# A mixture-of-experts layer: GpSimd's cast of the second weights put ahead of its scatter-adds, and gelu biases read without a copy

## The chip, the core and the metric

One core of a Trainium2 chip. The time is the device time of one execution in microseconds, the median over runs; lower is better. The core has engines that run side by side, each with its own queue of instructions in order: TensorE (PE, matmul), VectorE (DVE), ScalarE (ACT), GpSimd (POOL) and SyncE (SP, which here only issues loads and stores). They meet at semaphores.

## What is computed

A small adapter turns x with weights chosen by a condition, then a mixture of 8 experts, top 2 of 8, runs over T = 1024 tokens of 256 values with 160 places per expert and choice, and a shared expert is added:

```
xt = einsum('bct,bcd->bdt', x, w[conditions]).reshape(T, 256)
top_p, top_i = top_k(softmax(xt @ gate_w), 2)
for k in range(2):
    buf[e, pos] = xt                          # pos = place in expert e, dropped at 160 and over
    h = gelu(buf @ w1 + b1)                   # 256 -> 1024, per expert
    y = h @ w2 + b2 + gelu(buf @ wd) @ wu     # 1024 -> 256, and rank 32
    out += y[e, pos] * w[:, None]
out += 0.2 * (gelu(xt @ sw1 + sb1) @ sw2 + sb2 + gelu(xt @ swd) @ swu)
result = x + out.reshape(B, S, D)
```

## The kernel before

Float32 products are made of three matmuls in the fast fp32r type: every operand is split into a high part (a cast) and a low part (the value less the high part), and `three` multiplies high with high and high with low both ways. So all weights and activations pass through a cast on ScalarE or GpSimd and a subtraction on VectorE.

The kernel has a head (condition, gate, routing, shared expert, up to about 80 us) and then eight experts, one period each. Both choices of an expert are done together: its rows (320 places, 288 of them multiplied) lie in a scratch tensor `slot_rows`, filled by scatter (line 423). For expert e:

- **TensorE**: `hidden`, tiles 0 (rank 32) to 8, into three PSUM banks; after tile 2 (tile 1 for the last expert) `turn_results` of expert e-1; then `turn_slots` of expert e+1 (line 970), then `expert_out` (the last expert: `last_out`).
- **ScalarE**: two gelus for each tile (lines 526, 527), w1's casts for expert e+1, the turned slots' high part, half of w2's casts (line 470), the copies of y (line 561).
- **VectorE**: the low part of each tile (line 623); behind tile 2 the last chunk, chunk 3, of `w2_l` of expert e (line 599); behind tile 3 (tile 1 for the last expert) `weigh_rows` of expert e-1 into `y_row` (line 740), which first waits until the scatter-adds of expert e-2 have landed (`combined`), as `y_row` is there only once; then w1's low parts for e+1 (line 587), `wd` and `wu`, the slots' low part, chunks 0 to 2 of `w2_l`.
- **GpSimd**, `period` (line 428), the queue that is changed: `small_hi(e + 2)` casts `wd` and `wu` (lines 358, 363); `combine(e - 1)`, three scatter-adds of `y_row` into `out` (line 401); `side_data(e)`, five small operations that give the slots' weights `slot_w`, which `weigh_rows` reads, and target rows (lines 380 to 389), signalled by `slots_sided`; `set_bias(e + 1)` copies 8 columns of `bias_t` to `bias_now` (line 374); `w2_hi_part(e + 2)` casts chunks 2 and 3 of w2 (line 369), when its load has landed. Weights are numbered v = e + 1, since number 0 is the shared expert: `e + 2` in the code is the next expert's weights.
- **SyncE**, its queue strictly in order (lines 307 to 310): `load_first(e + 1)` w1, wd, wu, b2 once the raw ones are used; `load_slots(e)`, which waits for `slots_turned` and for `slots_sided` of the expert two before it, as `slot_in` has two buffers; `load_second(e + 1)` w2 (line 265), which waits until `w2_lo` has used all of `w2_raw`, of which there is one buffer.

Routing, shared expert and the loops of other engines are as printed.

Of the kernel before, what the change touches and what calls it, by code (L numbers as in the profile page):

```python
# [15 lines left out]
P = 128  # L16
# [4 lines left out]
E, K = 8, 2  # L21
# [3 lines left out]
SLOTS = K * CAP  # L25
SHARED_SCALE = 0.2
KD = D // P
NF = H // P
# [21 lines left out]
def build(nc, x, itok, cond_w, gate_w, w1, b1, w2, b2, wd, wu, sw1, sb1, sw2, sb2, swd, swu, out, slot_rows, cond_rows):  # L50
    with ExitStack() as ctx:
        def sb(name, shape, dt=F32):
            return ctx.enter_context(nc.sbuf_tensor(name, shape, dt))
# [4 lines left out]
        def sem(name):  # L58
            return ctx.enter_context(nc.semaphore(name))
# [31 lines left out]
        gate2 = sb("gate2", [P, KD, 2 * E], F32R)  # L91
        bias_rows = sb("bias_rows", [P, P])
        bias_t = sb("bias_t", [P, N_BIAS])
        bias_now = [sb(f"bias_now{i}", [P, NF]) for i in range(2)]
        less_high = sb("less_high", [P, 1])
        empty_row = sb("empty_row", [P, ROW])

# [52 lines left out]
        spare_out = sem("spare_out")  # L150
        dispatched = sem("dispatched")
        base_out = sem("base_out")
# [21 lines left out]
        scores_copied = sem("scores_copied")  # L174
        bias_turned = sem("bias_turned")
        bias_ready = sem("bias_ready")
        bias_set = sem("bias_set")
        route = sem("route")
        centred = sem("centred")
        expd_made = sem("expd_made")  # L180
# [19 lines left out]
        y_copied = sem("y_copied")  # L200
# [25 lines left out]
        def hid_count(u, j):  # L226
            return u * HT + (j + 1)
# [7 lines left out]
        def hid_bank(u, j):  # L235
            return hid_ring(u)[j % len(hid_ring(u))]
# [83 lines left out]
        def _(pool):  # L320
# [31 lines left out]
            def small_hi(v, par, waits=True):  # L352

                if waits:
                    pool.wait_ge(hid_made, hid_before(v))
                pool.wait_ge(wd_in, 16 * (v + 1))
                for g in range(3):
                    ins = pool.tensor_copy(wd_h[par][:, :, g, :], wd_raw[:, :, :])  # L358
                ins.then_inc(wd_hi, 1)
                if waits:  # L360
                    pool.wait_ge(y_made, y_before(v))
                pool.wait_ge(wu_in, 64 * (v + 1))
                pool.tensor_copy(wu_s[par][:, :], wu_raw[:, :]).then_inc(wu_hi, 1)

            def w2_hi_part(v, par):

                pool.wait_ge(w2_in, 16 * (v + 1))
                for c in range(ACT_W2, CHUNKS):
                    pool.tensor_copy(w2_h[par][:, c * FT:(c + 1) * FT, :],  # L369
                                     w2_raw[:, c * FT:(c + 1) * FT, :]).then_inc(w2_hi[1], 1)  # L370

            def set_bias(e, par):

                pool.tensor_copy(bias_now[par][:, :], bias_t[:, e * NF:(e + 1) * NF]).then_inc(bias_set, 1)

            def side_data(e, par):


                pool.wait_ge(slots_in[par], (e + (2 - par)) * 16)
                pool.tensor_copy(slot_w[par][:, :], slot_in[par][:, :, W_COL]).then_inc(slot_math, 1)  # L380
                pool.tensor_scalar(slot_free[:, :], slot_in[par][:, :, ID_COL], float(T), None,
                                   ALU.is_ge).then_inc(slot_math, 1)
                pool.wait_ge(slot_math, e * SIDE + 2)
                pool.tensor_tensor(slot_spare[:, :], slot_free[:, :], slot_local[:, :], ALU.mult).then_inc(slot_math, 1)
                pool.wait_ge(slot_math, e * SIDE + 3)
                pool.tensor_tensor(slot_row[:, :], slot_spare[:, :], slot_in[par][:, :, ID_COL],
                                   ALU.add).then_inc(slot_math, 1)
                pool.wait_ge(slot_math, e * SIDE + 4)
                pool.tensor_copy(slot_tok[par][:, :], slot_row[:, :]).then_inc(slots_sided, KD)

            def combine(e, par):

                pool.wait_ge(y_weighted, e * ST + 1)
                pool.wait_ge(slots_sided, (e + 1) * KD)
                if e > 0:
                    pool.wait_ge(combined, e * (16 * ST))
                for s in range(ST):
                    n = ST_ROWS[s]
                    if s > 0:
                        pool.wait_ge(y_weighted, e * ST + s + 1)  # L400
                    pool.indirect_dma_start(  # L401
                        out=out, out_offset=bass.IndirectOffsetOnAxis(ap=slot_tok[par][0:n, s:s + 1].bitcast(U32), axis=0),
                        in_=y_row[0:n, s, :], in_offset=None, bounds_check=T + SLOTS - 1,
                        compute_op=ALU.add).then_inc(combined, 16)
# [4 lines left out]
            for b in range(NT // 2):  # L409
                pool.wait_ge(rows_copied, b + 1)  # L410
                pool.tensor_copy(token_row[1][:, 2 * b:2 * b + 2, 0:D],
                                 token_row[0][:, 2 * b:2 * b + 2, 0:D]).then_inc(rows_twice, 1)
            pool.wait_ge(bias_ready, 1)
            set_bias(0, 0)
            small_hi(1, 1, waits=False)

            pool.wait_ge(rows_copied, NT // 2)
# [7 lines left out]
                        in_=token_row[k][:, t, :], in_offset=None, bounds_check=E * SLOTS - 1,  # L425
                        oob_is_err=False).then_inc(dispatched, 16)

            def period(e, par, combine_one=True, split=True, biases=True):
                if split:
                    small_hi(e + 2, par)  # L430
                if combine_one:
                    combine(e - 1, 1 - par)
                side_data(e, par)
                if biases:
                    if combine_one:
                        pool.wait_ge(y_copied, e * KD)
                    set_bias(e + 1, 1 - par)
                if split:
                    w2_hi_part(e + 2, par)

            period(0, 0, combine_one=False)
            pool.wait_ge(base_out, 32)
            pool.wait_ge(spare_out, 16)
            for e in range(1, E - 1):
                period(e, e % 2)
            period(7, 1, split=False, biases=False)
            combine(7, 1)


        @block.scalar  # L450
        def _(act):
# [5 lines left out]
            def w1_chunk(v, par, c):  # L457

                if c == 0:
                    act.wait_ge(w1_in, 16 * (v + 1))  # L460
                act.activation(w1_h[par][:, :, c * FC:(c + 1) * FC], w1_raw[:, :, c * FC:(c + 1) * FC],  # L461
                               ACT.Copy).then_inc(w1_hi, 1)

            def w2_chunk(v, par, c):

                if c == 0:
                    act.wait_ge(w2_in, 16 * (v + 1))
                    if v >= 2:
                        act.wait_ge(y_made, y_before(v))
                act.activation(w2_h[par][:, c * FT:(c + 1) * FT, :], w2_raw[:, c * FT:(c + 1) * FT, :],  # L470
                               ACT.Copy).then_inc(w2_hi[0], 1)
# [42 lines left out]
            def gelu_tile(u, j, n, bias):  # L514

                act.wait_ge(hid_made, hid_count(u, j))
                if u == 0 and j < 3:
                    pass
                else:
                    act.wait_ge(hid_split, hid_count(u, j) - 3)  # L520
                src = hid_bank(u, j)
                if j == 0:
                    act.activation(gelu_f[2 * RANK:3 * RANK, 0, 0:n], src[2 * RANK:3 * RANK, 0:n], ACT.Gelu)
                    act.activation(low_s[0:LOW, 0:n], src[0:LOW, 0:n], ACT.Gelu).then_inc(hid_gelu, 1)
                else:
                    act.activation(gelu_f[:, j % 3, 0:n], src[:, 0:n], ACT.Gelu, bias=bias(j - 1))  # L526
                    act.activation(hid_h[:, j - 1, 0:n], src[:, 0:n], ACT.Gelu, bias=bias(j - 1)).then_inc(hid_gelu, 1)  # L527

            def slots_hi_part():
                for k in range(KD):  # L530
                    act.activation(xs_h[:, k, :], turn_ps[k][:, 0:SLOTS], ACT.Copy).then_inc(slots_hi, 1)
# [11 lines left out]
            slots_hi_part()  # L543

            def period(e, par, split=True, turned=True):

                act.wait_ge(bias_set, e + 1)

                for j in range(HT):
                    gelu_tile(e + 2, j, SLOTS, lambda f: bias_now[par][:, f:f + 1])  # L550
                if split:
                    for c in range(CHUNKS):
                        w1_chunk(e + 2, par, c)
                        if c == 1:
                            act.wait_ge(slots_turned, e * KD + 2 * KD)
                            slots_hi_part()
                    for c in range(ACT_W2):
                        w2_chunk(e + 2, par, c)
                for m in range(KD if turned else 0):
                    act.wait_ge(y_made, 2 * HTILES + (e * KD + (m + 1)))  # L560
                    act.activation(y_t[:, m, :], y_ps[m][:, 0:SLOTS], ACT.Copy).then_inc(y_copied, 1)

            period(0, 0)
            for e in range(1, E - 1):
                period(e, e % 2)
            period(7, 1, split=False, turned=False)


# [481 lines left out]
```

## Time and profile before

| | us |
|---|---|
| median of 3 runs | 210.36 (210.09 to 210.44) |
| the profiled execution | 210.76 |
| its span, first to last instruction | 208.9 |

| engine | busy us | share of the span |
|---|---|---|
| TensorE | 191.0 | 91% |
| VectorE | 134.4 | 64% |
| ScalarE | 132.9 | 64% |
| GpSimd | 112.0 | 54% |

Times inside a trace are microseconds from the start of the span. A timeline row gives start, length, engine, line, operation, what it writes and reads, and in brackets how long the engine was idle before it and what ended that. A waits row gives who waited for whom. "Issue" is time in which an engine waited for nothing that the profile shows.

### The profile page before, as it was taken

The numbers are of one execution on the slowest core, as the hardware profiler recorded it, in microseconds if no ns is written. First come the engines' busy times: TensorE is split into PE (matmuls) and PEld (weight loads), VectorE is DVE, ScalarE is ACT, GpSimd is POOL, SyncE is SP. The second block draws the span as 40 slices with busy tenths as digits, with TensorE's granted clock in tenths as the row PEclk, the third lists the DMA queues.
The fourth block names the chain that finished last, engine by engine and source line by source line (L and its number), as shares of the span: only waits on it lengthen the run. The fifth ranks groups of instructions, "written<-read, shape, count | busy, mean of one in ns | idle before, by whom it ended". The sixth has DMA issues, their size and how long they took to land.

```text
span 208.9 us, 3977 instructions
## 1 busy us (share of the span) xinstructions
PE 191.0 (91%) x1409; PEld 183.1 (88%) x1409; DVE 134.4 (64%) x294; ACT 132.9 (64%) x283; POOL 112.0 (54%) x162
## 2 busy tenths in 40 slices
PE   6569999999999499999999999999999999999930
PEld 6567777998888499999999999999999999999920
DVE  4547489744852024695878869869869968968020
ACT  2247799903890106968949949949949859768000
POOL 6202304087872015001784894885876867948662
PEclk9969999999999799999999999999999999999995
DMA  5599972422221895017867867866787776600523
GB/s 178 166 300 321 221 259 50 173 80 78 102 100 57 222 350 183 3 20 275 224 107 237 218 147 217 209 194 198 171 232 202 129 258 220 90 1 6 60 32 38
DMA packets 27898, 33.04 MB, mean 158 GB/s; under 512 B 4554, under 2 KB 24772, under 8 KB 27876
## 3 DMA queue, kind: packets, MB, share of 16 engines
q1 hardware_dynamic: 23748, 27.31, 42.8%
q0 software_dynamic: 3760, 4.89, 14.4%
q10 hardware_dynamic: 368, 0.56, 0.9%
q8 instruction: 13, 0.21, 0.4%
q14 instruction: 9, 0.07, 0.1%
HBM read 23.96 MB, written 8.79 MB: 157 GB/s over the span
## 4 chain that ended last, share of the span: by engine, by line
POOL 28%; PE 24%; issue 19%; DVE 16%; DMA 8%; POOLq 1%; ACT 1%; SPq 1%; DVEq 0%
POOL out_rows L401 13%; POOL slot_w L380 6%; POOL slot_rows L423 5%; DVE w_l L599 5%; DVE y_row L740 4%; PE hid_ps L806 3%; PE hid_ps L808 3%; PE hid_ps L807 3%; DVE hid_l L623 3%; DMA gate_raw<-in_L_ffn_gate_w 2%; PE y_ps L806 2%; PE y_ps L808 2%; PE y_ps L807 2%; DMA out_rows<-y_row,slot_tok 2%; DMA slot_rows<-token_row,slot_i 2%
## 5 line engine op out<-in xcount | busy, mean ns | idle before, releaser
L401 POOL DMA_INDIRECT out_rows<-y_row,slot_tok x24 | 46.0, 1919 | 14.3 <-DVE y_row L740 6.7
L623 DVE TENSOR_TENSOR hid_l<-gelu_f,hid_h 128x320 fp32r<-128x320 f32 (+1 forms) x80 | 41.3, 531 | 13.6 <-ACT hid_h L527 12.7
L806 PE MATMUL hid_ps<-xs_h,w_h 128*128 128x288 f32 x128 | 38.2, 298 | 0.0
L808 PE MATMUL hid_ps<-xs_h,w_l 128*128 128x288 f32 x128 | 37.6, 294 | 0.0
L807 PE MATMUL hid_ps<-xs_l,w_h 128*128 128x288 f32 x128 | 37.6, 294 | 0.0
L526 ACT ACTIVATE gelu_f<-hid_ps,bias_now 128x320 f32<-128x320 f32 x64 | 35.0, 547 | 1.1 <-PE hid_ps L808 0.4
L527 ACT ACTIVATE hid_h<-hid_ps,bias_now 128x320 fp32r<-128x320 f32 x64 | 35.4, 553 | 0.0
L358 POOL CAST wd_h<-wd_raw 128x64 fp32r<-128x64 f32 x27 | 9.9, 404 | 45.8 <-DMA wd_raw<-in_L_ffn_wd 44.7
L599 DVE TENSOR_TENSOR w_l<-w_raw,w_h 128x512 fp32r<-128x512 f32 x36 | 26.3, 748 | 12.5 <-POOL w_h L369 11.8
L808 PE MATMUL y_ps<-hid_h,w_l 128*128 128x288 f32 x112 | 32.9, 294 | 0.0
L807 PE MATMUL y_ps<-hid_l,w_h 128*128 128x288 f32 x112 | 32.9, 294 | 0.0
L806 PE MATMUL y_ps<-hid_h,w_h 128*128 128x288 f32 x112 | 32.9, 294 | 0.0
L423 POOL DMA_INDIRECT slot_rows<-token_row,slot_i x16 | 17.9, 1121 | 11.8 <-issue 11.8
L807 PEld LDWEIGHTS hid_ps<-xs_l,w_h 128*128 128x128 f32 x128 | 24.0, 188 | 0.0
L806 PEld LDWEIGHTS hid_ps<-xs_h,w_h 128*128 128x128 f32 x128 | 24.0, 188 | 0.0
L808 PEld LDWEIGHTS hid_ps<-xs_h,w_l 128*128 128x128 f32 x128 | 24.0, 188 | 0.0
L587 DVE TENSOR_TENSOR w_l<-w_raw,w_h 128x512 fp32r<-128x512 f32 x36 | 23.4, 685 | 0.5 <-ACT w_h L461 0.3
L806 PE MATMUL y_ps<-w_h,hid_h 128*128 128x256 f32 x80 | 23.0, 287 | 0.0
L808 PE MATMUL y_ps<-w_h,hid_l 128*128 128x256 f32 x80 | 22.9, 286 | 0.0
L807 PE MATMUL y_ps<-w_l,hid_h 128*128 128x256 f32 x80 | 22.9, 286 | 0.0
L461 ACT ACTIVATE w_h<-w_raw 128x512 fp32r<-128x512 f32 x36 | 22.0, 702 | 0.0
L806 PEld LDWEIGHTS y_ps<-hid_h,w_h 128*128 128x128 f32 x112 | 21.0, 188 | 0.0
(182 smaller groups left out, 422.5 us busy)
## 6 DMA issues: line engine op xcount, KB each, us to landing
w_raw<-in_L_ffn_w SPq DMA_DIRECT2D x16, 1024.0 KB, 5.3
slot_rows<-empty_row SPq DMA_DIRECT2D x1, 2600.0 KB, 17.1
slot_in<-slot_rows SPq DMA_DIRECT2D x8, 260.0 KB, 3.7
x_in<-in_x SPq DMA_DIRECT2D x2, 512.0 KB, 4.4
w_raw<-in_L_ffn_sw SPq DMA_DIRECT2D x1, 1024.0 KB
out_rows<-base SPq DMA_DIRECT2D x2, 512.0 KB, 3.6
wu_raw<-in_L_ffn_wu SPq DMA_DIRECT2D x24, 32.0 KB
slot_in<-slot_rows SPq DMA_DIRECT2D x8, 65.0 KB, 3.8
```

What stands on the lines that cost most here:

```text
L380: pool.tensor_copy(slot_w[par][:, :], slot_in[par][:, :, W_COL]).then_inc(slot_math, 1)
L401: pool.indirect_dma_start(out=out, out_offset=bass.IndirectOffsetOnAxis(ap=slot_tok[par][0:n, s:s + 1].bitcast(U32), axis=0), in_=y_row[0: ...
L423: pool.indirect_dma_start(out=slot_rows, out_offset=bass.IndirectOffsetOnAxis(ap=slot_i[:, t, k:k + 1].bitcast(U32), axis=0), in_=token_ro ...
L461: act.activation(w1_h[par][:, :, c * FC:(c + 1) * FC], w1_raw[:, :, c * FC:(c + 1) * FC], ACT.Copy).then_inc(w1_hi, 1)
L526: act.activation(gelu_f[:, j % 3, 0:n], src[:, 0:n], ACT.Gelu, bias=bias(j - 1))
L527: act.activation(hid_h[:, j - 1, 0:n], src[:, 0:n], ACT.Gelu, bias=bias(j - 1)).then_inc(hid_gelu, 1)
L587: dve.tensor_tensor(w1_l[par][:, :, cols], w1_raw[:, :, cols], w1_h[par][:, :, cols].bitcast(F32), ALU.subtract).then_inc(w1_lo, 1)
L599: dve.tensor_tensor(w2_l[par][:, rows, :], w2_raw[:, rows, :], w2_h[par][:, rows, :].bitcast(F32), ALU.subtract).then_inc(w2_lo, 1)
L623: dve.tensor_tensor(hid_l[:, j - 1, 0:n], gelu_f[:, j % 3, 0:n], hid_h[:, j - 1, 0:n].bitcast(F32), ALU.subtract).then_inc(hid_split, 1)
L806: pe.matmul(out_ap, l_h, r_h, start=start, stop=False)
L807: pe.matmul(out_ap, l_h, r_l, start=False, stop=False)
L808: return pe.matmul(out_ap, l_l, r_h, start=False, stop=stop)
```

## The change

GpSimd's period is put in another order: small casts, w2's casts, then scatter-adds, then side data. The waits on the first store of `out` stand ahead of the scatter-adds of period 1 as before, but behind that period's casts. `set_bias`, `bias_now` and `bias_set` go: the gelus read `bias_t` directly, and ScalarE no longer waits at a period's start, nor GpSimd for `y_copied`.

```diff
@@ gpsimd
-            pool.wait_ge(bias_ready, 1)
-            set_bias(0, 0)
             small_hi(1, 1, waits=False)
@@
-            def period(e, par, combine_one=True, split=True, biases=True):
-                if split:
+            def period(e, par):
+                if e + 2 <= E:
                     small_hi(e + 2, par)
-                if combine_one:
+                    w2_hi_part(e + 2, par)
+                if e == 1:
+                    pool.wait_ge(base_out, 32)
+                    pool.wait_ge(spare_out, 16)
+                if e > 0:
                     combine(e - 1, 1 - par)
                 side_data(e, par)
-                if biases:
-                    if combine_one:
-                        pool.wait_ge(y_copied, e * KD)
-                    set_bias(e + 1, 1 - par)
-                if split:
-                    w2_hi_part(e + 2, par)
...
+            for e in range(E):
                 period(e, e % 2)
-            period(7, 1, split=False, biases=False)
-            combine(7, 1)
+            combine(E - 1, (E - 1) % 2)
@@ scalar
-                act.wait_ge(bias_set, e + 1)
                 for j in range(HT):
-                    gelu_tile(e + 2, j, SLOTS, lambda f: bias_now[par][:, f:f + 1])
+                    gelu_tile(e + 2, j, SLOTS, lambda f: bias_t[:, e * NF + f:e * NF + f + 1])
```

## Rows read from the trace of the kernel before

**Rows 1.** Page, section 1: busy us (share of the span) and instructions

```profile
PE 191.0 (91%) x1409; PEld 183.1 (88%) x1409; DVE 134.4 (64%) x294; ACT 132.9 (64%) x283; POOL 112.0 (54%) x162
```

**Rows 2.** Windows, the fifth period: busy of each engine, clock, DMA share, GB/s

```profile
127.70:142.70 15.00, 15.00 (x118) 15.00 (x117) 12.23 (x28) 12.16 (x29) 11.40 (x16) 1.00 0.74 196
```

**Rows 3.** Waits: engine and line waited for releaser: us in total, times, longest

```profile
DVE w_l L599 <- POOL w_h L369: 11.8, 6, 2.0
...
ACT gelu_f L523 <- POOL bias_now L374: 4.5, 6, 0.8
```

**Rows 4.** Chain of waits, last 22 us: start, length, what

```profile
194.44 4.25 DMA out_rows<-y_row,slot_tok
```

**Rows 5.** Timeline of GpSimd, one period: start, length, line, operation

```profile
172.85 1.21 POOL L358 CAST wd_h<-wd_raw 128x64 fp32r<-128x64 f32 x3 [2.09 <-DMA wd_raw<-in_L_ffn_wd]
...
174.99 2.31 POOL L401 DMA_INDIRECT out_rows<-y_row,slot_tok  x1 [0.59 <-DVE y_row L740]
...
179.71 1.69 POOL L401 DMA_INDIRECT out_rows<-y_row,slot_tok  x1 [0.31 <-issue]
180.89 2.45 POOL L380 COPY slot_w<-slot_in 128x3 f32<-128x3 f32 x1
...
184.35 0.19 POOL L389 CAST slot_tok<-slot_row 128x3 int32<-128x3 f32 x1
...
184.62 1.16 POOL L369 CAST w_h<-w_raw 128x512 fp32r<-128x512 f32 x2
```

**Rows 6.** Timeline of VectorE, same period and the end of it

```profile
172.67 0.69 DVE L599 TENSOR_TENSOR w_l<-w_raw,w_h 128x512 fp32r<-128x512 f32 x1
...
176.65 0.49 DVE L623 TENSOR_TENSOR hid_l<-gelu_f,hid_h 128x320 fp32r<-128x320 f32 x1 [0.34 <-ACT hid_h L527]
...
182.01 1.29 DVE L599 TENSOR_TENSOR w_l<-w_raw,w_h 128x512 fp32r<-128x512 f32 x2
185.26 1.07 DVE L599 TENSOR_TENSOR w_l<-w_raw,w_h 128x512 fp32r<-128x512 f32 x1 [1.96 <-POOL w_h L369]
...
187.28 0.48 DVE L740 TENSOR_SCALAR y_row<-y_ps,slot_w 128x256 f32<-128x256 f32 x1
```

**Rows 7.** Timeline of SyncE's queue, from 64 to 174 us: start, length, what

```profile
97.97 0.38 SPq L265 DMA_DIRECT2D w_raw<-in_L_ffn_w  x1
...
169.86 0.38 SPq L272 DMA_DIRECT2D slot_in<-slot_rows  x1
170.29 0.48 SPq L273 DMA_DIRECT2D slot_in<-slot_rows  x1
173.38 0.39 SPq L265 DMA_DIRECT2D w_raw<-in_L_ffn_w  x1
```

**Rows 8.** Windows of half a microsecond, behind the load of 173.38

```profile
177.50:178.00 0.50, 0.50 (x6) 0.50 (x5) 0.47 (x2) 0.50 (x2) 0.39 (x1) 1.00 1.13 305
178.00:178.50 0.50, 0.50 (x6) 0.50 (x5) 0.50 (x1) 0.50 (x2) 0.50 (x1) 1.00 1.03 115
```

**Rows 9.** Timeline of GpSimd, narrow windows: single small casts

```profile
172.85 0.60 POOL L358 CAST wd_h<-wd_raw 128x64 fp32r<-128x64 f32 x1 [2.09 <-DMA wd_raw<-in_L_ffn_wd]
...
173.84 0.23 POOL L358 CAST wd_h<-wd_raw 128x64 fp32r<-128x64 f32 x1
```

**Rows 10.** Timeline of GpSimd, end of the kernel

```profile
188.55 3.72 POOL L401 DMA_INDIRECT out_rows<-y_row,slot_tok  x1 [2.77 <-DVE y_row L740]
...
197.08 0.18 POOL L389 CAST slot_tok<-slot_row 128x3 int32<-128x3 f32 x1
199.99 1.66 POOL L401 DMA_INDIRECT out_rows<-y_row,slot_tok  x1 [2.73 <-DVE y_row L750]
...
203.81 1.43 POOL L401 DMA_INDIRECT out_rows<-y_row,slot_tok  x1 [0.30 <-issue]
```

**Rows 11.** Timeline of TensorE, turning of the next slots

```profile
176.08 0.82 PE L970 MATMUL turn_ps<-ident,slot_in 128*128 128x128 f32 x6
```

**Rows 12.** Line 272, load of slots: us from issue to landing

```profile
DMA to landing us min/median/max: 2.7/3.7/3.8
```

More of the change, by code:

```diff
@@ L93, in build @@
         bias_t = sb("bias_t", [P, N_BIAS])
-        bias_now = [sb(f"bias_now{i}", [P, NF]) for i in range(2)]
         less_high = sb("less_high", [P, 1])
@@ L176, in build @@
         bias_ready = sem("bias_ready")
-        bias_set = sem("bias_set")
         route = sem("route")
@@ L370, in w2_hi_part @@
                                      w2_raw[:, c * FT:(c + 1) * FT, :]).then_inc(w2_hi[1], 1)
-            def set_bias(e, par):
-                pool.tensor_copy(bias_now[par][:, :], bias_t[:, e * NF:(e + 1) * NF]).then_inc(bias_set, 1)
             def side_data(e, par):
@@ L426, in _ @@
                         oob_is_err=False).then_inc(dispatched, 16)
-            def period(e, par, combine_one=True, split=True, biases=True):
-                if split:
+            def period(e, par):
+                if e + 2 <= E:
                     small_hi(e + 2, par)
-                if combine_one:
+                    w2_hi_part(e + 2, par)
[3 more added lines that the diff above has]
+                if e > 0:
                     combine(e - 1, 1 - par)
                 side_data(e, par)
-                if biases:
-                    if combine_one:
-                        pool.wait_ge(y_copied, e * KD)
-                    set_bias(e + 1, 1 - par)
-                if split:
-                    w2_hi_part(e + 2, par)
[L441 to L444, printed above, removed]
+            for e in range(E):
                 period(e, e % 2)
-            period(7, 1, split=False, biases=False)
-            combine(7, 1)
+            combine(E - 1, (E - 1) % 2)
         @block.scalar
```

## The prediction, made before the changed kernel ran

> **What bounds the kernel now.** I read the page's busy times first: TensorE is at work for 191.0 us of a span of 208.9 [rows 1]. A share over the whole span hides stages, so next came the windows by stage: in an expert's period, 15.0 us long and repeated from 97.7 to 187.3, TensorE is busy for 15.00 of 15.00 us, while VectorE has 12.23, ScalarE 12.16 and GpSimd 11.40 [rows 2]. Inside a period there is nothing to win for any other engine. The table of waits names the two things that the change is aimed at: VectorE waits for GpSimd's cast of the second weights, 11.8 us in 6 waits, and ScalarE for `bias_now`, 4.5 us in 6 [rows 3]. Both waits lie beside a TensorE that never stops for them, so their 16.3 us are no part of the span. The chain of waits does run through GpSimd; that chain starts at the end, and in the periods it only shows who was released last, not that TensorE waited.
>
> Time can be won only behind 187.3, where the chain is real: `y_row` of expert 6 is weighed at 187.28 (W7 below), three scatter-adds follow, the last starts at 194.44, its rows land 4.25 us later, `y_row` is written again for expert 7, three more scatter-adds, the end [rows 4, 6, 10].
>
> **The biases.** Removed: eight copies of 128x8, about 0.2 us each (as the cast of `slot_tok` of that size [rows 5]), and ScalarE's wait. A gelu reads the same [128,1] column from `bias_t` instead of `bias_now`; same form, cost 0. ScalarE starts each period up to 0.8 us earlier [rows 3], under TensorE's cover: gain 0 in the periods, at most those 0.8 us in the last one, if W7 hung on it.
>
> **The cast moved ahead.** In a period GpSimd now does: `wd`/`wu` casts, three scatter-adds, side data, bias copy, two casts of `w2` [rows 5]. After: small casts, wait for `w2_raw`, two casts, scatter-adds, side data. The load of `w2_raw` goes out only when VectorE has used the old one (its chunk 3 ends at 173.36, the load is issued at 173.38 [rows 6, 7]), only 1.6 us ahead of the first scatter-add at 174.99 [rows 5]. So the casts cannot come early: everything queued behind them on GpSimd (scatter-adds, side data) now waits for a transfer that had been hidden.
>
> I count from the issue L of that load:
> - L to landing 5.0 us: the 1 MB issued at 173.38 holds the DMA queues at 305 GB/s up to 178.0, then the rate falls to 115 [rows 8]. Bounds 4.8 and 5.5 (slots are issued right ahead of it now).
> - two casts, 2.0 us. Undisturbed they take 1.16 [rows 5]. They would start in VectorE's run of subtractions (w1 chunks, from about L+4.6). There a 128x64 cast took 0.60 against 0.23 us a moment later, as if it waited for the end of one VectorE instruction each [rows 9]; with two such waits of some 0.4 us, 2.0. Bounds 1.2 and 2.5.
> - first to third scatter-add, start to start: 4.7 us (174.99 to 179.71). Bounds 3.8 (199.99 to 203.81, all quiet) and 5.9 (188.55 to 194.44) [rows 4, 5, 10].
> - third scatter-add's start to the end of the side data: 4.8 us in a period (179.71 to 184.54), 2.8 at the end of the kernel where VectorE is idle (194.44 to 197.26) [rows 4, 5, 10]. In the new place VectorE goes through an expert's first tiles, 0.49 us each with some 0.3 us of waiting between them, as in [rows 6]: 3.3, nearer the quiet row.
> - side data to next L: 0.9 us. SyncE's queue is in order: `load_slots` waits for `slots_sided`, and `load_second` stands behind it. Its two issues start at 169.86 and 170.29, the second takes 0.48 [rows 7].
>
> Sum: 5.0 + 2.0 + 4.7 + 3.3 + 0.9 = 15.9 us from one L to the next, a closed loop over SyncE and GpSimd. It is longer than TensorE's 15.0. Before, the loop had no 5.0 and no 2.0 in it, because the scatter-adds did not wait for the load. That is what this change turns from hidden work into the bound.
>
> How it adds up: L1 is 97.97. Then L2 = 97.97 + 15.9 = 113.87 (now 113.36, one period of 15.0 before the next), and L6 = 113.87 + 4 x 15.9 = 177.47, against 173.38 [rows 7]. The scatter-adds of expert 5 then start at 184.5, the third at 189.2, and land 4.25 later at 193.4. W7 waits for that landing (`combined`), since `y_row` is single. Before, this landing was at 179.7 + 4.25 = 184.0 and W7 at 187.28 hung on other things. So W7 moves by 6.1 us.
>
> From W7 to the end I keep the 21.6 us of before. It holds a first scatter-add of 3.72 us against 2.31 in the periods [rows 5, 10]; it may shrink by up to 1.4, it doesn't grow. TensorE's own last work follows W7, as VectorE's remaining tiles stand behind the weighing.
>
> **Who notices on the way.** `load_slots` is now issued by the late side data. TensorE turns the slots 2.7 us after L now (176.08 against 173.38 [rows 7, 11]); the slot load is issued 0.9 before L and lands 3.7 us (2.7 to 3.8) after its issue [rows 12], the second one 0.4 later, so at about L+3.2. TensorE therefore stands 0.5 us plus L's delay in the first period and then once per period about what the loop has over 15.0. This is the same delay, not a second one. The granted clock is 1.00 in the periods [rows 2], the 2.4 GHz level; I take no change of it for gaps of a microsecond.
>
> What is removed is then: VectorE's 1.96 us wait for the cast goes (11.8 in all), ScalarE's wait goes, and neither is worth anything.
>
> **The rivals.**
> 1. The tail alone. If casts, scatter-adds and side data take their quiet values, the loop is 4.8 + 1.2 + 3.8 + 2.8 + 0.9 = 13.5, under 15.0: no period grows. L6 stays 173.38 and the landing of expert 5 comes 4.8 + 1.2 + 3.8 + 4.25 = 14.05 to, with a loop just at 15.0, 15.2 us later, at 187.4 to 188.6; W7 is late by 0.1 to 1.3 us. Time 210.5 to 211.7, taken as 211.2. For it: the wait frees VectorE of a 1.07 us subtraction that ran beside the cast [rows 6]. Against: no period shows quiet values for all three.
> 2. Faster. VectorE no longer waits for the cast at 185.26, so W7 could be up to 0.8 us earlier (as ScalarE's first tile), if expert 5's rows have landed by 186.5, which means 13.1 us after L6. The quiet sum is 14.05. It needs each value below its lowest row: 209.6 to 210.2. Likewise "it does nothing": 210.4.
> 3. The casts are held by the whole VectorE run, not by one instruction. The copy of `slot_w` behind the third scatter-add ended at 183.34, after 2.45 us, and VectorE's unbroken run at 183.30, while a copy of that size takes 0.2 [rows 5, 6]. If that holds for the casts, they start at about L+9.9 (183.30 against 173.38) and the loop is 11.1 + 4.7 + 3.3 + 0.9 = 20.0: L6 = 197.97, landing at 218.0, W7 later by 30.7 us, 241 us. Against: the small casts in [rows 9], which got through one at a time.
> The Trainium skill's GPSIMD Engine Reference, section Key points, says that GpSimd shares its SBUF interfaces with VectorE and contends with VectorE instructions that have two SBUF inputs. It doesn't say how long GpSimd is kept out; taken as full exclusion it gives rival 3, about 241 us, and taken as sharing in turn it gives the forecast. The rows on casts agree with turns, the row on `slot_w` with exclusion.
>
> **How the numbers follow.** Forecast 72%: 210.36 + 6.1, rounded to 216.5 us. The profiled execution took 210.76, its span is 208.9, 1.86 outside it; it is 0.4 above the median of the runs, and I add to the median. Its own range: with a loop of 15.3, L6 = 174.5 and W7 = 189.9 (+2.6, 213.0); with 17.0, L6 = 183.0 and landing at 199.8 (+12.5, 222.9). Rival 1: 12%. Rival 2 with no effect: 10%, half of it faster. Rival 3 and everything over 223: 6%. The low end takes in most of rival 1: 211.0 to 222.9. A measurement here can tell about 0.2% from no change; faster 0.05, same 0.06, slower 0.89.
>
> **What would show it.** Right: GpSimd's cast of `w2` waits for the DMA of `w_raw` some 4 us in each of six periods; VectorE's `y_row` waits for the landing of `out_rows` in periods 3 to 7; TensorE waits for `slot_in`; L265 is issued about 15.9 us apart. Wrong in size: casts of 0.6 us each, or L265 still 15.0 apart (rival 1), or casts that end with VectorE's run (rival 3). Wrong altogether: the scatter-adds start within 3 us of L, or the last `y_row` of expert 6 is at 187 or before.

## The result: slower, by the loop that was forecast, and twice as far

The changed kernel takes 223.18 us (median of four runs, 222.38 to 228.71) against 210.4 us of the kernel before, measured beside it: ratio 1.0622, 95% interval 1.0566 to 1.0679. The forecast was 216.5 us with a range up to 222.9; sign and mechanism were right, the size was not. In this document medians are over all runs of a kernel and ratios over its fast ones alone, as some executions take a few us more at a lower granted clock.

The profiled execution of the changed kernel (called after in what follows) took 222.38 us, its span is 220.5. The page, busy times and the first groups:

```profile
span 220.5 us, 3969 instructions
PE 194.7 (88%) x1409; PEld 185.4 (84%) x1409; DVE 136.6 (62%) x294; ACT 134.6 (61%) x283; POOL 101.2 (46%) x154
...
L367 POOL CAST w_h<-w_raw 128x512 fp32r<-128x512 f32 x14 | 11.8, 871 | 38.3 <-DMA w_raw<-in_L_ffn_w 38.3
```

Against [rows 1], GpSimd has 10.8 us less work and TensorE 3.7 us more; the span is 11.6 us longer. No engine got busier by that much: the time is waiting. The last line says whose: GpSimd stood 38.3 us in front of the casts, for the load of raw w2. The table of waits of after (who waited for whom: us, times, longest), beside [rows 3]:

```profile
POOL w_h L367 <- DMA w_raw<-in_L_ffn_w: 38.3, 7, 7.2
...
PE turn_ps L953 <- DMA slot_in<-slot_rows: 10.7, 6, 2.9
...
DVE y_row L723 <- DMA out_rows<-y_row,slot_tok: 6.7, 5, 2.9
...
SPq L269 <- POOL slot_tok L383: 23.6, 5, 6.4
```

The two waits that the change was aimed at are gone. In their place are the load in front of the casts, TensorE in front of its slots, `y_row` in front of its landing, and SyncE's queue, which waits for the side data in five periods. SyncE's timeline shows what comes of it (start, length, line; L253 is w1, L270 and L271 are the slots, L263 is w2):

```profile
99.21 0.39 SPq L263 DMA_DIRECT2D w_raw<-in_L_ffn_w  x1
109.25 0.37 SPq L253 DMA_DIRECT2D w_raw<-in_L_ffn_w  x1
...
114.65 0.38 SPq L270 DMA_DIRECT2D slot_in<-slot_rows  x1
115.07 0.48 SPq L271 DMA_DIRECT2D slot_in<-slot_rows  x1
115.59 0.60 SPq L263 DMA_DIRECT2D w_raw<-in_L_ffn_w  x1
...
132.76 0.59 SPq L263 DMA_DIRECT2D w_raw<-in_L_ffn_w  x1
...
149.35 0.58 SPq L263 DMA_DIRECT2D w_raw<-in_L_ffn_w  x1
...
166.84 0.59 SPq L263 DMA_DIRECT2D w_raw<-in_L_ffn_w  x1
...
183.95 0.59 SPq L263 DMA_DIRECT2D w_raw<-in_L_ffn_w  x1
```

From the first to the last L263 it is 84.74 us for five periods, 16.95 each; before it was 173.38 - 97.97 = 75.41, 15.08 each [rows 7]. One period on GpSimd's timeline:

```profile
122.75 1.63 POOL L367 CAST w_h<-w_raw 128x512 fp32r<-128x512 f32 x2 [6.33 <-DMA w_raw<-in_L_ffn_w]
124.55 1.90 POOL L395 DMA_INDIRECT out_rows<-y_row,slot_tok  x1 [0.17 <-issue]
126.75 1.56 POOL L395 DMA_INDIRECT out_rows<-y_row,slot_tok  x1 [0.30 <-issue]
128.62 1.43 POOL L395 DMA_INDIRECT out_rows<-y_row,slot_tok  x1 [0.30 <-issue]
129.54 0.70 POOL L374 COPY slot_w<-slot_in 128x3 f32<-128x3 f32 x1
...
131.55 0.19 POOL L383 CAST slot_tok<-slot_row 128x3 int32<-128x3 f32 x1
```

The load issued at 115.59 lets the casts start at 122.75; at 131.74 the side data ends; at 131.81 SyncE issues the slots, at 132.76 the next w2. The loop is closed, as the chain of the prediction has it.

Where the 11.6 us of span are: the head before the first slot load, whose code is the same but for one copy, took 68.69 us in this execution and 67.34 in that of before (1.35 us). It took 65.7 to 68.7 in the traces of this study, and 65.74 in after_yrow, whose code up to there is that of after, so it is spread and no effect of the change. From the first slot load to L6 it is 9.2 us more, from L6 to W7 1.8 more, from W7 to the end 0.8 less.

### The profile page after: what moved, and what is told of

Read it like the earlier page. It is cut to its first block, busy times and chain, and to the rows that moved or that the text cites. A ratio compares the mean times of both kernels' runs of the same rounds, so it can differ in the third digit from the quotient of the medians.

```text
span 220.5 us, 3969 instructions
## 1 busy us (share of the span) xinstructions
PE 194.7 (88%) x1409; PEld 185.4 (84%) x1409; DVE 136.6 (62%) x294; ACT 134.6 (61%) x283; POOL 101.2 (46%) x154
## 4 chain that ended last, share of the span: by engine, by line
issue 29%; POOL 24%; PE 22%; DMA 12%; DVE 6%; ACT 4%; POOLq 1%; SPq 1%; DVEq 0%
POOL out_rows L395 12%; POOL slot_rows L415 5%; DMA out_rows<-y_row,slot_tok 3%; DMA gate_raw<-in_L_ffn_gate_w 3%; DMA slot_in<-slot_rows 3%; DMA wd_raw<-in_L_ffn_wd 2%; PE y_ps L791 2%; PE y_ps L789 2%; PE hid_ps L789 2%; PE y_ps L790 2%; PE hid_ps L791 2%; PE hid_ps L790 2%; ACT gelu_f L512 2%; POOL wd_h L356 2%; PE hid_ps L810 2%
## 5 line engine op out<-in xcount | busy, mean ns | idle before, releaser
L512 ACT ACTIVATE gelu_f<-hid_ps,bias_t 128x320 f32<-128x320 f32 (+1 forms) x77 | 43.7, 568 | 9.6 <-DVE hid_l L606 4.9
L395 POOL DMA_INDIRECT out_rows<-y_row,slot_tok x24 | 41.1, 1713 | 9.1 <-issue 6.1
L513 ACT ACTIVATE hid_h<-hid_ps,bias_t 128x320 fp32r<-128x320 f32 (+1 forms) x77 | 43.8, 569 | 0.0
L367 POOL CAST w_h<-w_raw 128x512 fp32r<-128x512 f32 x14 | 11.8, 871 | 38.3 <-DMA w_raw<-in_L_ffn_w 38.3
L582 DVE TENSOR_TENSOR w_l<-w_raw,w_h 128x512 fp32r<-128x512 f32 x36 | 25.2, 730 | 1.6 <-ACT w_h L456 1.6
L570 DVE TENSOR_TENSOR w_l<-w_raw,w_h 128x512 fp32r<-128x512 f32 x36 | 25.1, 731 | 0.5 <-ACT w_h L447 0.3
L789 PE MATMUL y_ps<-w_h,hid_h 128*128 128x256 f32 x80 | 23.9, 299 | 0.0
L791 PE MATMUL y_ps<-w_h,hid_l 128*128 128x256 f32 x80 | 23.7, 297 | 0.0
L790 PE MATMUL y_ps<-w_l,hid_h 128*128 128x256 f32 x80 | 23.7, 297 | 0.0
L356 POOL CAST wd_h<-wd_raw 128x64 fp32r<-128x64 f32 x27 | 7.8, 327 | 34.3 <-DMA wd_raw<-in_L_ffn_wd 32.9
L447 ACT ACTIVATE w_h<-w_raw 128x512 fp32r<-128x512 f32 x36 | 21.3, 664 | 0.0
```

What stands on the lines that cost most here:

```text
L395: pool.indirect_dma_start(out=out, out_offset=bass.IndirectOffsetOnAxis(ap=slot_tok[par][0:n, s:s + 1].bitcast(U32), axis=0), in_=y_row[0: ...
L570: dve.tensor_tensor(w1_l[par][:, :, cols], w1_raw[:, :, cols], w1_h[par][:, :, cols].bitcast(F32), ALU.subtract).then_inc(w1_lo, 1)
L582: dve.tensor_tensor(w2_l[par][:, rows, :], w2_raw[:, rows, :], w2_h[par][:, rows, :].bitcast(F32), ALU.subtract).then_inc(w2_lo, 1)
L789: pe.matmul(out_ap, l_h, r_h, start=start, stop=False)
L790: pe.matmul(out_ap, l_h, r_l, start=False, stop=False)
L791: return pe.matmul(out_ap, l_l, r_h, start=False, stop=stop)
```

## The experiments

L is an issue of the w2 load; "period" is the mean distance of the six L from 97 us on, or of the first six weighings of `y_row` where that is said. Each ratio is to the kernel before, run on the same chip, where its median was 209.6 to 210.4.

| run | median us | ratio, 95% interval | period us |
|---|---|---|---|
| changed kernel | 223.18 | 1.062 (1.057 to 1.068) | 16.95 |
| bias_only | 210.06 | 1.003 (0.998 to 1.007) | 15.0 (weighings) |
| order_only | 230.55 | 1.096 (1.089 to 1.104) | 18.2 |
| side_first | 227.05 | 1.074 (1.062 to 1.085) | 17.5 |
| second_first_same_wait | 238.8 | 1.133 (1.126 to 1.140) | 20.3 |
| one_cast_on_act | 220.31 | 1.052 (1.041 to 1.063) | 16.5 |
| casts_on_act | 219.67 | 1.046 (1.039 to 1.055) | 16.6 |
| after_yrow | 221.19 | 1.055 (1.048 to 1.062) | 17.2 |
| side_first_yrow | 213.82 | 1.016 (1.011 to 1.022) | 15.1 |
| w2_double | 208.59 | 0.994 (0.989 to 0.998) | 15.0 (weighings) |
| w2_double_old_order | 209.95 | 0.988 (0.980 to 0.996) | 15.0 (weighings) |
| both_double | 209.1 | 0.994 (0.990 to 0.998) | 15.0 (weighings) |
| yrow_double | 209.94 | 1.000 (0.996 to 1.004) | 15.0 (weighings) |

### Each part by itself

```diff
# bias_only, to the kernel before
-                act.wait_ge(bias_set, e + 1)
-                    gelu_tile(e + 2, j, SLOTS, lambda f: bias_now[par][:, f:f + 1])
+                    gelu_tile(e + 2, j, SLOTS, lambda f: bias_t[:, e * NF + f:e * NF + f + 1])
# order_only, to the kernel before
                     small_hi(e + 2, par)
+                    w2_hi_part(e + 2, par)
...
                     set_bias(e + 1, 1 - par)
-                if split:
-                    w2_hi_part(e + 2, par)
```

> The change's bias part alone: the gelus read bias_t, no copy, no bias_set; GpSimd's old order is kept. Theory (all of the loss is the order of GpSimd's queue): 210.2 us, within 0.2% of before. Rival (the head, which ended 1.2 us later in the changed kernel's profile, or the wider table read by ScalarE, costs something): 211 to 212.

> The change's order alone: casts of w2 ahead of the scatter-adds, bias copies kept behind the side data. Theory: as the changed kernel, 223 us, issues of the w2 load some 17 us apart. Rival (the two parts work together, for instance through the start of ScalarE's tiles): more than 1 us off 223.

The biases alone give 1.003 (0.998 to 1.007): nothing that can be told from no change, as forecast, and no cost of the wider table. The order alone is not 223 but 230.55: the expectation missed by 7 us, on the side of its rival. Waits and SyncE's queue of order_only:

```profile
ACT gelu_f L523 <- POOL bias_now L374: 24.6, 6, 5.4
...
PE hid_ps L806 <- ACT low_s L524: 15.4, 6, 3.8
...
SPq L265 <- DVE w_l L599: 18.8, 7, 3.1
```

```profile
112.26 0.38 SPq L272 DMA_DIRECT2D slot_in<-slot_rows  x1
112.68 0.48 SPq L273 DMA_DIRECT2D slot_in<-slot_rows  x1
116.23 0.39 SPq L265 DMA_DIRECT2D w_raw<-in_L_ffn_w  x1
```

Behind the side data now stands the bias copy, and ScalarE's first tile waits for it (24.6 us in all, against 4.5 in [rows 3]). VectorE's last chunk of w2 stands behind the low part of tile 2, and the next load waits for the chunk (the last of these lines): it goes 4.0 us after the slots (112.26 to 116.23) instead of 0.9. So the biases' part, which alone is worth nothing, is worth some 7 us under the new order: it takes a second wait off the loop. The halves of the change can't be added up from runs of each.

### The link over SyncE

```diff
# second_first_same_wait, to the changed kernel
                 load_first(e + 1)
+                sp.wait_ge(slots_turned, (e - 1) * KD)
+                sp.wait_ge(slots_sided, (e - 1) * KD)
+                load_second(e + 1)
                 load_slots(e, e % 2)
-                load_second(e + 1)
```

> The changed kernel with SyncE's two loads swapped behind the same waits: w2 first, the slots behind it. Theory (the 6 to 7 us from issue to landing of w2, against 5.0 before, come from the slot load right ahead of it in the queue): the casts start 5.0 to 5.4 us after the issue; but the slots then land about 6.2 us after it, TensorE turns them late, and the period becomes some 18.4: 230 us. Rival (the load is slow for another reason): 6 to 7 us still.

The casts start 5.3 to 6.0 us after L (5.5 in the next two lines; mean 5.6), against 6.2 to 7.2 us in periods 2 to 6 of after (mean 6.7). So about 1.1 us of the load's time goes with the slot load that stands right ahead of it in the queue. order_only points the same way: there the slots are issued 3 to 4 us ahead of w2, and the casts start 5.2 to 5.5 us after L. It isn't the whole of it: in side_first, with the slots issued 1.4 to 3.4 us ahead, it took 5.5 to 6.8 us, and two issues with the same lead of 3.1 us took 5.5 and 6.8.

```profile
118.30 0.39 SPq L263 DMA_DIRECT2D w_raw<-in_L_ffn_w  x1
```

```profile
123.77 1.63 POOL L369 CAST w_h<-w_raw 128x512 fp32r<-128x512 f32 x2 [8.03 <-DMA w_raw<-in_L_ffn_w]
```

The slots come late instead, TensorE waits 23.7 us for them in all, and the whole is 238.8, 9 us over the expectation: the periods are 20.3 us, not the 18.4 that it names. A part of that miss is the clock. Windows of the same run (span of the window, busy of TensorE, ..., granted clock, DMA share, GB/s):

```profile
121.50:124.50 3.00, 0.00 (x0) 0.00 (x0) 2.29 (x5) 2.20 (x5) 0.73 (x2) 1.00 0.83 273
125.00:128.00 3.00, 3.00 (x14) 3.00 (x15) 2.34 (x7) 1.66 (x4) 2.53 (x3) 0.51 0.15 13
```

TensorE did nothing for 3.4 us (121.45 to 124.88), and in the 3 us from 125.0 on it was granted 0.51, close to the 1.2 GHz level: 14 matmuls where 3 us hold some 24 at full clock (118 in 15.0 us, [rows 2]).

### The second loop

```diff
# side_first, to the changed kernel
-                if e > 0:
-                    combine(e - 1, 1 - par)
+                if e > 1:
+                    pool.wait_ge(combined, (e - 1) * (16 * ST))
                 side_data(e, par)
+                if e > 0:
+                    combine(e - 1, 1 - par)
```

> The changed kernel with the five side-data operations put between the casts and the scatter-adds (with a wait for scatter-adds that landed long before). Theory (a closed loop: load of w2, casts, scatter-adds, side data, release of the slot load, next load of w2): the loop loses its scatter-adds, 4 us, and falls to some 12, so TensorE's 15.0 decides again; only the last landing stays late, 212 us. Rival (the periods grow because scatter-adds and y_row are late, not because side data is): 218 to 223.

227.05 us: the rival's side, and slower than the changed kernel. The forecast of 212 was wrong. SyncE no longer waits for the side data, and still the periods are long, because a wait that lay beside the first loop now ends last (side_first, the waits):

```profile
DVE y_row L725 <- DMA out_rows<-y_row,slot_tok: 18.3, 6, 6.1
...
ACT gelu_f L514 <- DVE hid_l L608: 16.4, 6, 5.9
```

The side data puts the scatter-adds 3 us further back; they land beside the next 1 MB load (the third one started at 130.46, `y_row` was free at 136.27, 5.8 us later, against 3.1 for the last one of after, 196.58 to 199.67). VectorE stands before `y_row`, behind it the tiles, behind them ScalarE and TensorE. If that is a second loop, two buffers for `y_row` must open it, and in the changed kernel itself they must do little:

```diff
# after_yrow and side_first_yrow: two buffers, the second on the stored base rows
-        y_row = sb("y_row", [P, ST, D])
+        y_rows = [sb("y_row", [P, ST, D]), base[:, 0:ST, :]]
...
-                    dve.wait_ge(combined, e * (16 * ST))
+                    dve.wait_ge(combined, (e - 1) * (16 * ST))
```

> Side data ahead of the scatter-adds, as in side_first (227 us), and two buffers for y_row, so that VectorE doesn't wait for the landing of the last scatter-adds. Theory (side_first opened the loop over the slot load, but a second loop, load of w2, casts, scatter-adds, landing, y_row, TensorE's next tiles, took its place): with both open TensorE's 15.0 us decide and the whole takes 211 us. Rival (only one loop exists, and something else made side_first slow): 218 or more.

> The changed kernel with two buffers for y_row only. Theory (in the changed kernel the loop over side data and the slot load is the one that decides, the wait of y_row lies beside it): periods stay near 17.0 us, only the two weighings at the end leave the chain, 220 to 222 us. Rival (y_row's wait makes the periods long): 216 or less.

Both came out that way. With only `y_row` doubled the changed kernel stays at 17.2 us from L to L (one of the five turns took 19.6, the others 16.4 to 16.7) and 221.19 us. With both loops open the periods are TensorE's again (15.1), and 227.05 falls to 213.82; the 2.8 us over the expected 211 lie in the tail, where from W7 to the end it is 24.7 us against 21.6, as GpSimd comes to the last scatter-adds late. So the changed kernel hangs on the loop over side data and slots, and beside it stands another that would make a period as long (17.5 us in side_first, against 16.95). Opening one of them alone buys 2 us or nothing, opening both buys the periods back.

### Taking links out of the loop

> The changed kernel with three of the four w2 casts on ScalarE, one on GpSimd (before: two and two). Theory (closed loop): each period is one cast shorter, 0.9 us, and the last landing too: 223.2 less 6 times 0.9, about 217.8. Rival (what counts is the wait for the load and what it does to TensorE, not GpSimd's time behind it): 222 to 223.

> The changed kernel with all four w2 casts on ScalarE; GpSimd only keeps the wait for the load ahead of its scatter-adds. Theory: the loop is 6.5 (load) + 4.1 + 3.4 + 1.1 = 15.1, so about TensorE's 15.0, if ScalarE has room for two more casts (1.2 us of some 2 us idle): 212 us. Rival (ScalarE becomes the bound): above 216.

The edit is one number, the count of w2's chunks that ScalarE casts (`ACT_W2 = 2` becomes 3, or 4). One cast less shortened the period by 0.5 us, not 0.9, and two less by 0.4. The total of one_cast_on_act says little: its four runs took 217.85, 219.17, 221.45 and 225.81 us at granted clocks of 0.970, 0.981, 0.960 and 0.953, and the expected 217.8 is near the first two. For casts_on_act it is plain: 219.67 where the theory had 212, on the side of its rival (above 216). The rival's reason, ScalarE as the bound, doesn't hold. The loop still closes over GpSimd, as the means over its five turns show:

| step | after | one_cast_on_act | casts_on_act |
|---|---|---|---|
| L to the first cast, or to the scatter-adds | 6.5 | 6.6 | 7.1 |
| casts | 1.8 | 0.9 | none |
| first to third scatter-add | 4.0 | 4.3 | 5.1 |
| third scatter-add to the end of the side data | 3.6 | 3.7 | 3.4 |
| side data to next L | 1.0 | 1.0 | 1.0 |
| sum | 16.95 | 16.5 | 16.6 |

Most of what the casts gave back went into the wait ahead of the scatter-adds and into the scatter-adds. GpSimd in casts_on_act, and VectorE beside it:

```profile
120.28 4.57 POOL L395 DMA_INDIRECT out_rows<-y_row,slot_tok  x1 [6.42 <-DMA w_raw<-in_L_ffn_w]
...
138.16 3.71 POOL L395 DMA_INDIRECT out_rows<-y_row,slot_tok  x1 [7.29 <-DMA w_raw<-in_L_ffn_w]
```

```profile
121.43 1.90 DVE L582 TENSOR_TENSOR w_l<-w_raw,w_h 128x512 fp32r<-128x512 f32 x3
...
138.46 1.89 DVE L582 TENSOR_TENSOR w_l<-w_raw,w_h 128x512 fp32r<-128x512 f32 x3
```

Without casts in front, the first scatter-add takes up to 4.6 us; behind a cast it took 1.7 to 1.9 in after. The lines show what the long ones have in common. VectorE's unbroken run of subtractions (no gap of 0.15 us in it) ends at 123.33, the scatter-add at 124.85; the next run ends at 140.35, the scatter-add at 141.87: 1.52 us later both times. Over all traces of this study 14 scatter-adds took more than 3 us, and each ended 1.4 to 1.6 us after the end of such a run (in side_first, 4.29 us long, after the last of w2's subtractions in it). So a long one looks like one that is held until VectorE pauses. Which ones are held was not settled: 1.66 and 2.14 us stand in the same run, and no experiment moved VectorE's work away. A link taken out of the loop was so filled for the most part by the next one.

### Taking the load out of the loop

```diff
# w2_double, to the changed kernel; v = 2, 4, 6, 8 lie on the tokens' second copy
-                sp.wait_ge(w2_lo, v * CHUNKS)
-                sp.dma_start(w2_raw[:, :, :], w2_v[v - 1]).then_inc(w2_in, 16)
+                if v == 2:
+                    sp.wait_ge(dispatched, 16 * NT * K)
+                else:
+                    sp.wait_ge(w2_lo, max(v - 1, 1) * CHUNKS)
+                sp.dma_start(w2_src(v)[:, :, :], w2_v[v - 1]).then_inc(w2_ins[w2_buf(v)], 16)
...
+                load_second(e + 1)
                 load_first(e + 1)
                 load_slots(e, e % 2)
-                load_second(e + 1)
```

> The changed kernel with two buffers for the raw w2 (the second one lies on a copy of the tokens that is no longer used) and its load issued at the head of SyncE's turn, almost a period early. Theory (the load between two steps of GpSimd's queue is what closed the loop): the cast waits for nothing, periods of 15.0 us, the cast off VectorE's path at the end: 209.8 us, at most 0.3% under before. Rival (the cast ahead of the scatter-adds costs by its own 1.8 us): 211 to 213.

208.59 us, ratio 0.994 (0.989 to 0.998): the new order with its load a period early is 6.5% faster than with the load in the loop (223.18), and no slower than before. Windows of it:

```profile
157.20:172.20 15.00, 15.00 (x118) 15.00 (x117) 12.23 (x28) 12.20 (x29) 9.70 (x13) 1.00 0.76 195
172.20:184.95 12.75, 12.75 (x101) 12.75 (x101) 10.57 (x25) 9.96 (x23) 9.36 (x13) 1.00 0.24 28
```

TensorE never stops in these periods, as in [rows 2], and of GpSimd's 38.3 us in front of the casts 2.0 are left, in one wait. The casts and their place in the queue are the same as in after, so neither cost the time: the load in front of them did. The second buffer and the earlier issue came together in this edit; what each is worth alone was not run.

What the new order is then worth by itself:

> The old order of GpSimd's queue (casts behind the side data) with gelus from bias_t, two buffers of raw w2 and the early load, as in w2_double (208.6 us). Theory (the early load alone is worth nothing in the old order, where the casts stand behind the scatter-adds; w2_double's gain comes from the casts' new place): 210.0 us, within 0.3% of before. Rival (the gain is the early load's): 208.6.

By the totals this can't be said: 0.988 (0.980 to 0.996) and 0.994 (0.989 to 0.998) overlap, and the first rests on two runs (206.73 and 209.12 us; the other two took 210.77 and 211.6). The forecast of no difference to before isn't borne out by that interval, nor refuted by so few runs. The traces say where to look. From the weighing of expert 5 to the end of the span it is 208.9 - 173.72 = 35.2 us before, 35.3 in bias_only (173.52 to 208.8) and 35.2 in w2_double_old_order (173.73 to 208.9), all with the old order; it is 33.0 in w2_double (172.16 to 205.2) and 33.3 in both_double (175.22 to 208.5), with the new one. In both of these VectorE weighs expert 6 12.8 us after expert 5 (184.95 in w2_double), against 13.6 before and 13.4 in the other two, as its subtraction doesn't wait for the cast; and the first scatter-add behind it takes 2.92 us against 3.72:

```profile
186.22 2.92 POOL L408 DMA_INDIRECT out_rows<-y_row,slot_tok  x1 [3.50 <-DVE y_row L736]
```

So with the early load the new order gives some 2 us, at the tail alone, in two traces against three. The profiled executions differ by more (206.99 us in w2_double, 210.77 in w2_double_old_order) because of the head as well: the first slot load is issued at 65.91 us, behind a granted clock of 1.00, in w2_double, and at 67.53, behind 0.97, in the other.

> The bias part alone plus two buffers for y_row (the second one on the stored base rows). Theory (behind the last period the chain waits for the landing of expert 6's rows before y_row is written again, but the scatter-adds of expert 7 must wait for the same landing and TensorE's last rows come 1.5 us behind it): at most 1.3 us better, 209.0 us. Rival: no difference, as TensorE's last rows decide.

> w2_double plus two buffers for y_row. Theory (its last periods run at TensorE's pace; at the end TensorE's last rows decide): 208.4 us, no more than 0.2% under w2_double, some 0.7% under before. Rival (the wait of y_row is on the chain at the end): 207.3.

Two buffers for `y_row` alone: 1.000 (0.996 to 1.004), the rival; in both_double 0.994 (0.990 to 0.998), the same as w2_double, so neither the 208.4 nor the rival's 207.3 can be told from its 209.1. At the end TensorE's last rows and the landing of expert 6's scatter-adds, for which those of expert 7 must wait anyway, come last. The three kernels with two buffers of raw w2 are the fastest of this study, w2_double by 0.6% over before, and are not told apart by their totals.

## Why the prediction was right in kind and short in size

- **What bounds it**: right. TensorE's 15.0 us hid everything; bias_only confirms that ScalarE's wait was worth nothing, and the removed waits of [rows 3] brought nothing.
- **The load between two steps of GpSimd's queue closes a loop over SyncE**: right, and shown by taking it out (w2_double).
- **The terms of the loop**: means over its five turns in after, and as predicted:

| step | predicted | measured |
|---|---|---|
| L to the start of the casts | 5.0 (4.8 to 5.5) | 6.5 (5.3 to 7.2) |
| casts | 2.0 | 1.8 |
| first to third scatter-add | 4.7 | 4.0 |
| third scatter-add to the end of the side data | 3.3 | 3.6 |
| side data to next L | 0.9 | 1.0 |
| sum | 15.9 | 16.95 |

The step that failed is the first term, "L to landing 5.0 us", bounds 4.8 and 5.5; it measured 6.5. I took the load's time from a load with nothing right ahead of it (the second slot load was issued 3.1 us before it [rows 7, 8]) and gave it an upper bound of 5.5, though the same part of the text says that the slots would be issued right ahead of it. In the first period, where they were not (slots at 96.12, w2 at 99.21), it took 5.33; later 6.2 to 7.2. With the two loads swapped it was 5.3 to 6.0. The slot load goes with 1.1 us of the 1.5; the rest was not traced. The other terms were off by 0.1 to 0.7 us each way and took 0.5 us off the miss between them.

- **Why a miss of 1 us became 5**: the loop counts above TensorE's 15.0. Predicted 0.9 above, measured 1.95, a factor of two on a term that is taken five times: 5 x 1.05 = 5.3 us. L6 came out 9.2 us late from the first slot load on, where 4.1 was forecast; W7, 1.8 more (forecast 2.0); the end -0.8 (0, at most -1.4). 9.2 + 1.8 - 0.8 = 10.2, against 6.1. The profile's remaining 1.35 us are the head's spread; the medians lie 12.8 apart, and 1.2 us of that are not placed by a single trace.
- **Right by luck**: the way from L6 to W7. Forecast were 15.95 us, measured 15.75 (183.95 to 199.70), but the casts started 1.2 us later than forecast and the rows landed 3.1 us after the third scatter-add began, not 4.25.
- **The upper end** was reckoned with a loop of 17.0 and came to 222.9; the loop was 16.95, and the measured 223.18 lies just behind it. Loop and tail explain 10.2 us, which is 220.6; what carries the median past the upper end is the head's spread and the unplaced 1.2 us, which no run here ties to the mechanism. One row is misread in the text, to no effect: L2 before was 113.33, not 113.36.
- **The place of the landing**: half right. I named `y_row`'s landing only as what moves W7, and "the same delay, not a second one" for TensorE. side_first shows that it closes a loop of its own, hidden by the first.
- **Casts held by one VectorE instruction or by its whole run** (rival 3): the casts of after took 1.2 to 2.2 us a pair, in turns, as forecast. In the line of the cast group above one 128x512 cast takes 871 ns on average, against a median of 611 before. But two single casts in other traces were held much longer. In side_first_yrow (GpSimd, then VectorE):

```profile
165.88 3.62 POOL L368 CAST w_h<-w_raw 128x512 fp32r<-128x512 f32 x1
```

```profile
167.12 1.90 DVE L585 TENSOR_TENSOR w_l<-w_raw,w_h 128x512 fp32r<-128x512 f32 x3
```

  The cast ends at 169.50, 0.48 us after VectorE's unbroken run (169.02). In after_yrow one of 2.67 us ends at 121.94, again 0.48 us after a run (121.46); it stands in the turn of 19.6 us. So what rival 3 describes does happen, in single turns, and the text was wrong to take the small casts as speaking against it altogether; what decides between the two was not found. The Trainium skill's GPSIMD Engine Reference, section Key points, speaks of contention with VectorE instructions that have two SBUF inputs: these casts agree with it. Beside such subtractions they took about half as much time again on average, and in the two cases above they were kept out until the run was over.
- **Rivals 1 and 2** took 4.8 us for the first term, and no turn has less than 5.3. But even with 6.5 in it the sum of quiet values is 15.2, just over TensorE's 15.0; the casts (1.8 for 1.2) and the side data (3.6 for 2.8) make most of the rest up to 16.95.

## What to carry to other kernels

An operation moved ahead in an in-order queue brings its waits with it: before moving it, ask when its input arrives, not when its engine is free, and list what stands behind it. If one of those releases the input's next load, the queue and the load form a loop whose length, with every transfer that stands ahead of the load in its own queue, is to be set against the period of the bounding engine; what it has over is paid once per turn, so an error in one term is multiplied. Opening one loop shows little if a second one is as long; the cure was to take the transfer out with a second buffer.

## What the runs showed of the hardware that was not expected

- Behind a 1 MB load issued 0.9 us after a 260 KB and a 65 KB load, the waiting cast started 6.2 to 7.2 us after the issue (after); 5.3 to 6.0 when the load went ahead of them (second_first_same_wait).
- A scatter-add of 128 rows of 1 KB took GpSimd between 1.55 and 4.57 us. The 14 of more than 3 us each ended 1.4 to 1.6 us after the end of a run of VectorE's subtractions; two casts of 2.67 and 3.62 us (0.61 undisturbed) ended 0.48 us after one. Which operations are held this long and which pass is open.
- After 3.4 us without a matmul TensorE was granted 0.51, close to the 1.2 GHz level, from 125 to 128 us of second_first_same_wait; a gap of some 1.7 us in after (133.2 to 134.9) left it at 1.00.
